# Mamba-2 block and feed-forward on one core: decay mask on GpSimd, differences for four heads at once, scores copied by ScalarE, and a new order on all engines

## The chip, the cores and the metric

The kernel runs on one core of a Trainium2 chip. The metric is the device time of one execution in microseconds (us), given as the median of the runs. The core has five engines that take their instructions in order from queues of their own and wait for each other by semaphores: TensorE (PE, with its weight loads PEld), VectorE (DVE), ScalarE (ACT), GpSimd (POOL) and SyncE (SP), which here only issues DMA transfers.

## The reference, cut to what matters

Input u is 4 x 1024 x 256, float32. Two layers, each with a residual:

```python
x = x + layernorm(mamba2(layernorm(x)))      # 8 heads of 64, state 128, conv of 4 taps
x = x + layernorm(ffn(layernorm(x)))         # width 2048, 4-bit weights, gelu(gate) * up, then down
# inside mamba2, for each chunk:
seg  = cs[..., :, None] - cs[..., None, :]   # cs: running sum of dt * A
Lmat = exp(where(tril, seg, -inf))           # decay matrix of each head
Y_diag = einsum(C, B, Lmat, x * dt)
states = einsum(B, exp(cs_last - cs), x * dt)
Y_off  = einsum(C, previous states, exp(cs))
y = (Y_diag + Y_off + x * D) * silu(z);  y = y * rsqrt(mean(y * y) + eps) * norm_weight
```

The kernel takes chunks of 128 time steps. For a chunk it needs, for every head, the matrix exp(cs[l] - cs[s]) for s <= l and zero elsewhere, multiplied by the scores B[s].C[l].

## The kernel before

**Tiling.** The 4096 time steps are treated in blocks of 512, shifted by half a block, so that there are 9 blocks (`NBLK`), the first and the last of them half. A block has two halves (j = 0, 1) of 256 steps, a half two tiles (q = 0 to 3 in the block) of 128. Iteration i runs the Mamba part of block i and the feed-forward part of block i - 1 interleaved.

**Order.** Every engine has its own written list of steps: `FIRST` for the start (blocks 0 and 1 and the half of block 2), `ORDER` for the iterations 2 to 8, `LAST` for the last feed-forward. A step is `name:k`; a trailing `<` means that it belongs to the block before (all feed-forward steps in `ORDER`), `>` to the next. `drive` walks the lists. No engine can leave its order, so a step that waits holds up everything written behind it on that engine.

**Feed-forward steps** (16 of each, n = 0 to 15): `gu:n` on TensorE makes the gate and the up product of 128 hidden columns (six matmuls of 512 columns each), `gelu:n` on ScalarE (L710) reads the gate bank, `inter:n` on VectorE (L999) multiplies it with the up bank, `split:n` on ScalarE (L717) and on GpSimd (L588) makes the high and low parts, `dn:n` on TensorE adds the down product (12 matmuls). Gate and up banks turn in a ring of three: gate n takes the bank that `inter:n-2` has read, up n the bank that `gelu:n-1` has read.

**Mamba steps of a half**, as far as the change touches them:
- `ip` projections and `taps` (ScalarE, L660 and L663), `conv` (VectorE, L881 to L901: a copy of the history, six multiply-adds at L890, a copy back), `silu` (ScalarE, L670). conv:1 with silu:1 gives x, conv:2 with silu:2 gives B and C of the first half, 4 and 5 those of the second.
- `softplus` gives dt * A; `cs` (TensorE, L1123) sums it along time; `decays` (VectorE, L843) copies the result to `csr`; SyncE stores that as rows in memory (L485) and spreads them over all partitions into `lmat`, one transfer of 512 KB for each tile (L493); `ct` (TensorE, L1127) transposes it; `sums` (VectorE, L850 to L855) collects `ct_`.
- `decay_sums:k` (four heads each) subtracts cs[s] in place in `lmat` and takes the minimum with 0 (VectorE, L864; for three of the four halves in `FIRST` on ScalarE, L643: 12 of 64 groups). `decay_matrix:k` (ScalarE, L652) takes the exponential. `exps` (L634) takes that of `ct_`.
- `gb` (TensorE, L1152) makes the scores and transposes B. `gb_copy` on VectorE (L873) copies the scores, multiplied by the 0/1 triangle `upto`; `gb_copy` on ScalarE (L685) copies the transposed B. `decayed_products:q` (VectorE, L909) multiplies `lmat` by the scores of the tile; this also zeroes what lies above the diagonal.
- `xtr`, `xdt` (x * dt), `yo` (TensorE, L1172: from the state), `yd:q` (TensorE, L1182: the diagonal part; waits for `decayed_products:q` and `xdt:q`), `st` (L1191), `ydiag`, `yt`, `out`, `stats2`, `ln2`, `x1n`.

ScalarE loads a table when it changes between gelu, silu and exponential (ACT_TABLE_LOAD).

Of the kernel before, what the change touches and what calls it, by code (L numbers as in the profile page):

```python
# [47 lines left out]
TINY = 1e-30  # L48

# [1233 lines left out]
```

## Time and profile before

| | us |
|---|---|
| median of 3 runs | 967.86 (967.83 to 968.83) |
| the profiled execution, its own time | 965.19 |
| its span, first to last instruction | 963.1 |
| TensorE busy (weight loads) | 880.5 (767.2) |
| VectorE busy | 751.7 |
| ScalarE busy | 614.1 |
| GpSimd busy | 355.0 |
| mean granted TensorE clock | 0.972 of full speed |

All times of single instructions come from the one profiled execution. An iteration of `ORDER` shows as a period of 109.4 us: its first gate product starts at 179.2, 288.3, 397.9 us and so on. In a timeline row the first number is the start, the second the time from the first instruction's start to the last one's end, `x6` the number of instructions merged; the brackets give the idle time in front and who ended it.

### The profile page before, as it was taken

To read this page: it belongs to the slowest core of one execution; us is meant where nothing else is said; L and a number is where in the kernel's file an instruction comes from. 1 tells how busy PE (TensorE), PEld (TensorE's weight loads), DVE (VectorE), ACT (ScalarE), POOL (GpSimd) and SP (SyncE) were. 2 spreads that over 40 slices of the span, in tenths; PEclk is the share of its full clock that TensorE was granted. 3 is DMA by queue.
4 is the path that set the end of the run, shared out by engine and by line. 5 is a ranking of instruction groups with operands and counts; after the bars stand their busy time and mean duration, and the time that the engine had idled before them with its cause. 6 is when DMAs were issued, how large, how long until landed. Compare 5 with 4: busy or idle time off the path is not lost.

```text
span 963.1 us, 17495 instructions
## 1 busy us (share of the span) xinstructions
PE 880.5 (91%) x6304; PEld 767.2 (80%) x6304; DVE 751.7 (78%) x2031; ACT 614.1 (64%) x1031; POOL 355.0 (37%) x342
## 2 busy tenths in 40 slices
PE   3256979999999999999999999999999999999987
PEld 3136878978897887988898897888888898888886
DVE  5989889877888697887978788787978878786232
ACT  5767777866749394765858385774858485673222
POOL 2030515253342516243442515243442525344323
PEclk9579999999999999999999999999999999999999
DMA  7502010200101010100102010110102010010000
GB/s 228 178 1 56 1 56 2 67 1 21 37 13 66 1 56 2 57 21 13 45 12 67 1 56 1 36 43 13 45 13 67 1 56 1 23 45 1 1 23 11
DMA packets 19205, 34.57 MB, mean 36 GB/s; under 512 B 2480, under 2 KB 11440, under 8 KB 19120
## 3 DMA queue, kind: packets, MB, share of 16 engines
q1 hardware_dynamic: 18256, 33.44, 10.8%
q8 instruction: 50, 0.82, 0.3%
q14 instruction: 35, 0.29, 0.1%
q10 hardware_dynamic: 864, 0.03, 0.1%
HBM read 29.14 MB, written 4.33 MB: 35 GB/s over the span
## 4 chain that ended last, share of the span: by engine, by line
PE 63%; DVE 15%; ACT 13%; issue 5%; POOL 3%; DMA 1%; SPq 0%; POOLq 0%; ACTq 0%; DVEq 0%
PE fb L1082 28%; PE db L1082 14%; PE mb L1082 10%; DVE xc L890 3%; PE mb L1191 3%; ACT L710 3%; PE mb L1182 2%; POOL hl L588 2%; ACT hid L710 2%; PE mb L1172 2%; ACT xc L670 2%; PE mb L1197 1%; ACT xc L663 1%; DVE st L1007 1%; ACT lmat L652 1%
## 5 line engine op out<-in xcount | busy, mean ns | idle before, releaser
L588 POOL TENSOR_TENSOR hl<-hid,hl 128x512 fp32r<-128x512 f32 (+1 forms) x144 | 182.7, 1273 | 336.1 <-ACT hl L717 336.1
L1082 PE MATMUL fb<-x1t,wg 128*128 128x512 f32 (+1 forms) x864 | 215.9, 386 | 3.2 <-DVE x1t L993 2.7
L1082 PE MATMUL fb<-x1t,wu 128*128 128x512 f32 (+1 forms) x864 | 203.2, 371 | 16.3 <-ACT hid L710 16.3
L1082 PE MATMUL db<-wd,hl 128*128 128x256 f32 x1536 | 217.5, 291 | 0.7 <-POOL hl L588 0.7
L1082 PEld LDWEIGHTS db<-wd,hl 128*128 128x128 f32 x1536 | 196.2, 191 | 14.7 <-issue 9.8
L1082 PEld LDWEIGHTS fb<-x1t,wu 128*128 128x128 f32 x864 | 150.6, 190 | 51.5 <-ACT hid L710 25.4
L1082 PEld LDWEIGHTS fb<-x1t,wg 128*128 128x128 f32 x864 | 147.6, 191 | 36.4 <-issue 11.6
L710 ACT ACTIVATE hid<-fb 128x512 f32<-128x512 f32 (+1 forms) x144 | 78.5, 550 | 135.1 <-PE fb L1082 119.5
L890 DVE SCALAR_TENSOR_TENSOR xc<-raw,cw,xc 128x256 f32<-128x256 f32 x288 | 135.7, 539 | 6.8 <-ACT xc L663 4.8
L999 DVE TENSOR_TENSOR hid<-fb,hid 128x512 f32<-128x512 f32 (+1 forms) x144 | 90.1, 626 | 60.7 <-PE fb L1082 34.4
L558 POOL TENSOR_TENSOR rs<-ve,neg_half 128x1 f32<-128x1 f32 (+2 forms) x89 | 61.9, 696 | 175.6 <-DVE ve L792 68.5
L717 ACT ACTIVATE hl<-hid 128x512 fp32r<-128x512 f32 (+1 forms) x144 | 82.1, 580 | 56.9 <-DVE hid L999 40.1
L710 ACT ACT_TABLE_LOAD x65 | 83.4, 1283 | 25.3 <-POOL hl L588 24.5
L1082 PE MATMUL mb<-xnt,wi 128*128 128x256 f32 x576 | 79.5, 289 | 13.8 <-ACT sz L678 9.0
L1082 PEld LDWEIGHTS mb<-xnt,wi 128*128 128x128 f32 x576 | 74.3, 195 | 15.3 <-issue 14.7
L567 POOL TENSOR_TENSOR xdd<-xdt,ex 128x512 f32<-128x512 f32 x32 | 34.4, 1076 | 82.4 <-ACT ex L634 64.9
L1082 PE MATMUL mb<-wi,xnt 128*128 128x264 f32 (+1 forms) x384 | 52.3, 285 | 0.2 <-ACT xc L663 0.2
L1082 PE MATMUL mb<-wo,yt 128*128 128x256 f32 x384 | 51.6, 283 | 0.0
L864 DVE TENSOR_SCALAR lmat<-lmat,ct_ 128x128 f32<-128x128 f32 x208 | 51.6, 316 | 0.0
L1082 PEld LDWEIGHTS mb<-wo,yt 128*128 128x128 f32 x384 | 47.9, 189 | 1.8 <-issue 1.0
L663 ACT ACTIVATE xc<-mb,cb,cw 128x256 f32<-128x256 f32 x96 | 49.2, 573 | 0.0
L1082 PEld LDWEIGHTS mb<-wi,xnt 128*128 128x128 f32 x384 | 48.3, 189 | 0.4 <-issue 0.4
(141 smaller groups left out, 1294.1 us busy)
## 6 DMA issues: line engine op xcount, KB each, us to landing
lmat<-rows SPq DMA_DIRECT2D x32, 512.0 KB, 4.5
xin<-in_u SPq DMA_DIRECT2D x16, 256.0 KB, 2.7
out<-xb SPq DMA_DIRECT2D x16, 256.0 KB, 2.3
wg_raw<-in_packed SPq DMA_DIRECT2D x4, 256.0 KB, 12.4
wg_raw<-in_scales SPq DMA_DIRECT2D x4, 256.0 KB
...
```

What stands on the lines that cost most here:

```text
L558: pool.tensor_tensor(dst, src, neg_half[:, 0:src.shape[1]], ALU.pow).then_inc(s["rstd" + name], 1)
L567: pool.tensor_tensor(per_head(xdd[:]), per_head(xdt[:]), spread_heads(ex[:, q // 2, 1, q % 2, :]), ALU.mult).then_inc(s["xdd"], 1)
L588: pool.tensor_tensor(hl[:, hs, n % 2, 1, :], hid[:, hs, n % 2, :], hl[:, hs, n % 2, 0, :].bitcast(F32), ALU.subtract).then_inc(s["lo"], 1)
L663: last = act.activation(xc[:, ct, :], ps[:, e, :], ACT.Identity, bias=cb[:, ct:ct + 1], scale=cw[:, ct, TAPS - 1:TAPS])
L670: act.activation(xc[:, 2 * pr:2 * pr + 2, :], xc[:, 2 * pr:2 * pr + 2, :], ACT.Silu).then_inc(s["xc"], 1)
L710: act.activation(hid[:, halves(f), n % 2, :], by_half(f_bank["gate", n], f), ACT.Gelu_apprx_tanh).then_inc(s["gelu"], 1)
L717: act.activation(hl[:, halves(f), n % 2, 0, :], hid[:, halves(f), n % 2, :], ACT.Copy).then_inc(s["hi"], 1)
L864: last = dve.tensor_scalar(lmat[:, c, h0 + h, :], lmat[:, c, h0 + h, :], ct_[:, 0, r:r + 1], 0.0, ALU.subtract, ALU.min)
L890: ins = dve.scalar_tensor_tensor(out=xc[:, ct, :], in0=raw[:, slot, e, tap:tap + SUB], scalar=cw[:, ct, tap:tap + 1], in1=xc[:, ct, :], op ...
L999: dve.tensor_tensor(hid[:, halves(f), n % 2, :], by_half(f_bank["up", n], f), hid[:, halves(f), n % 2, :], ALU.mult).then_inc(s["inter"], 1)
L1082: last = pe.matmul(ps, lhs(a, k), rhs(b, k), start=start and n == 0, stop=stop and n == len(todo) - 1, skip_group_check=check)
L1191: pe.matmul(m_bank["st", q][:], gb[:, 2 + c, :], xdd[:], start=True, stop=True).then_inc(s["st"], 1)
```

## The change

- `mask:q`, new on GpSimd, for each tile: waits for the tile's spread rows and writes -1e30 into `lmat` where s > l (columns 0 to 126 of all 8 heads, in place, affine_select).
- `decay_sums` on VectorE: one tensor_tensor for four heads in place of four tensor_scalar; no minimum any more. It and the ScalarE form wait for the mask.
- VectorE's `gb_copy` is gone: ScalarE copies the scores unmasked together with the transposed B, 512 columns. `decayed_products` waits for that copy.
- The lists of all engines in `ORDER` and `FIRST` are new, and TensorE's and ScalarE's in `LAST`.

```diff
+FAR = -1e30
...
 ORDER = {
     "pe": """
-        gu:0< gu:1< cs:0 gu:2< ct:0 dn:0< gu:3< xtr:0 gu:4< dn:1< gb:0 dn:2< gu:5< yo:0 yd:0 dn:3< st:0 gu:6<
-        yt:0 xtr:1 dn:4< out:0 yo:1 dn:5< yd:1 st:1 gu:7< xt:1 yt:1 gu:8< ip:3 out:1 z:3 z:4 dn:6< gu:9< dn:7<
-        ip:4 cs:1 ip:5 gu:10< ct:1 z:5 gu:11< gu:12< dn:8< gb:1 yo:2 dn:9< xtr:2 xt:0> gu:13< dn:10< yd:2 dn:11<
-        st:2 yt:2 xtr:3 gu:14< out:2 yo:3 dn:12< yd:3 st:3 gu:15< yt:3 dn:13< x1t:0 out:3 z:0> z:1> dn:14<
+        gu:0< cs:0 gu:1< gu:2< dn:0< ct:0 gu:3< xtr:0 gb:0 yo:0 dn:1< yd:0 dn:2< gu:4< st:0 yt:0 xtr:1 gu:5<
+        out:0 dn:3< yo:1 gu:6< yd:1 gu:7< st:1 xt:1 dn:4< yt:1 ip:3 gu:8< out:1 z:3 z:4 dn:5< ip:4 gu:9< cs:1
+        ip:5 dn:6< ct:1 dn:7< gu:10< z:5 gu:11< gb:1 yo:2 xtr:2 dn:8< dn:9< gu:12< xt:0> yd:2 st:2 dn:10< gu:13<
+        yt:2 xtr:3 gu:14< dn:11< out:2 yo:3 dn:12< yd:3 gu:15< st:3 yt:3 dn:13< x1t:0 out:3 z:0> z:1> dn:14<
         dn:15< ip:0> x1t:1 ip:1> z:2> ip:2>""",
     "act": """
-        gelu:0< gelu:1< split:0< silu:0 gelu:2< silu:1 gate:2 split:1< split:2< gelu:3< silu:2 gelu:4< exps:0
-        decay_matrix:0 decay_matrix:1 decay_matrix:2 split:3< split:4< gb_copy:0 decay_matrix:3 gelu:5< split:5<
-        yt_split:0 square:0 gelu:6< gelu:7< yt_split:1 split:6< xn_split:1 split:7< taps:3 square:1 gelu:8<
-        gate:3 gate:4 dt_bias:1 gelu:9< split:8< taps:4 taps:5 gelu:10< split:9< gate:5 gelu:11< silu:3 silu:4
-        silu:5 decay_matrix:4 decay_matrix:5 split:10< gb_copy:1 exps:1 decay_matrix:6 gelu:12< split:11<
-        xn_split:0> decay_matrix:7 square:2 gelu:13< yt_split:2 split:12< gelu:14< split:13< gelu:15< split:14<
-        square:3 yt_split:3 split:15< dt_bias:0> gate:0> x1_split:0 gate:1> x1_split:1 taps:0> taps:1> taps:2>""",
+        gelu:0< gelu:1< split:0< gelu:2< silu:0 silu:1 split:1< gate:2 silu:2 decay_matrix:0 decay_matrix:1
+        gb_copy:0 split:2< exps:0 gelu:3< square:0 gelu:4< yt_split:0 split:3< decay_matrix:2 decay_matrix:3
+        split:4< gelu:5< gelu:6< split:5< xn_split:1 gelu:7< yt_split:1 split:6< square:1 taps:3 gelu:8<
+        dt_bias:1 split:7< gate:3 gate:4 taps:4 gelu:9< taps:5 split:8< split:9< gelu:10< silu:3 silu:4 silu:5
+        gate:5 gelu:11< exps:1 gb_copy:1 split:10< decay_matrix:4 decay_matrix:5 split:11< gelu:12< xn_split:0>
+        decay_matrix:6 gelu:13< yt_split:2 square:2 decay_matrix:7 split:12< split:13< gelu:14< gelu:15<
+        split:14< yt_split:3 split:15< square:3 dt_bias:0> x1_split:0 gate:0> taps:0> x1_split:1 gate:1> taps:1>
+        taps:2>""",
     "dve": """
-        inter:0< decays:0 inter:1< conv:1 inter:2< conv:2 sums:0 xdt:0 decay_sums:0 inter:3< decay_sums:1
-        inter:4< gb_copy:0 decay_sums:2 decay_sums:3 decayed_products:0 stats1:1 yoff:0 ydiag:0 inter:5<
-        decayed_products:1 state:0 yt_split:0 xdt:1 stats2:0 xn:1 yoff:1 ln2:0 ydiag:1 inter:6< inter:7< state:1
-        yt_split:1 xn_split:1 stats2:1 dt_bias:1 ln2:1 conv:3 softplus:1 inter:8< stats1:0> decays:1 inter:9<
-        conv:4 inter:10< xn:0> conv:5 sums:1 inter:11< decay_sums:4 decay_sums:5 decay_sums:6 gb_copy:1
-        decayed_products:2 xdt:2 yoff:2 inter:12< x1n:0 xn_split:0> decay_sums:7 ydiag:2 decayed_products:3
-        x1n:1 state:2 yt_split:2 xdt:3 inter:13< stats2:2 yoff:3 inter:14< ln2:2 ydiag:3 state:3 yt_split:3
-        inter:15< stats2:3 x1n:2 dt_bias:0> ln2:3 softplus:0> x1n:3 fin:0< x1_split:0 x1_split:1 conv:0> ln4:0<""",
+        decays:0 inter:0< conv:1 inter:1< conv:2 sums:0 decay_sums:0 decay_sums:1 inter:2< xdt:0
+        decayed_products:0 stats1:1 yoff:0 ydiag:0 inter:3< decay_sums:2 state:0 yt_split:0 xdt:1 inter:4< xn:1
+        decay_sums:3 stats2:0 decayed_products:1 yoff:1 ln2:0 inter:5< ydiag:1 state:1 inter:6< xn_split:1
+        yt_split:1 inter:7< conv:3 stats2:1 dt_bias:1 ln2:1 softplus:1 conv:4 decays:1 inter:8< inter:9<
+        stats1:0> conv:5 sums:1 inter:10< decay_sums:4 decay_sums:5 inter:11< x1n:0 xdt:2 decay_sums:6 xn:0>
+        decayed_products:2 yoff:2 xn_split:0> ydiag:2 decay_sums:7 inter:12< state:2 yt_split:2 xdt:3 inter:13<
+        decayed_products:3 stats2:2 inter:14< yoff:3 ln2:2 ydiag:3 inter:15< x1n:1 yt_split:3 x1n:2 state:3
+        stats2:3 dt_bias:0> ln2:3 softplus:0> x1n:3 fin:0< x1_split:0 x1_split:1 conv:0> ln4:0<""",
     "pool": """
-        split:0< split:1< split:2< xdt:0 split:3< yoff:0 split:4< stats1:1 split:5< stats2:0 xdt:1 yoff:1
-        split:6< split:7< ln2:0 stats2:1 stats1:0> split:8< split:9< split:10< xdt:2 yoff:2 split:11< ln2:1
-        split:12< xdt:3 stats2:2 yoff:3 split:13< ln2:2 split:14< split:15< stats2:3 ln2:3 fin:0<""",
+        split:0< mask:0 mask:1 split:1< split:2< xdt:0 yoff:0 split:3< stats1:1 stats2:0 split:4< xdt:1 yoff:1
+        ln2:0 split:5< split:6< stats2:1 split:7< split:8< split:9< stats1:0> mask:2 mask:3 ln2:1 split:10<
+        split:11< xdt:2 yoff:2 split:12< xdt:3 stats2:2 split:13< yoff:3 split:14< ln2:2 split:15< stats2:3
+        ln2:3 fin:0<""",
...
+            def mask(i, par, q):
+
+                c = q % 2
+                pool.wait_ge(rows_spread[c], 16 * halves_before(i, q // 2) + 16)
+                pool.affine_select(out=lmat[:, c, :, 0:CH - 1], in_=lmat[:, c, :, 0:CH - 1], compare_op=ALU.is_ge,
+                                   fill=FAR, base=0, pattern=[[0, HEADS], [1, CH - 1]],
+                                   channel_multiplier=-1).then_inc(s["masked"], 1)
+
...
                 c, h0 = k // 2 % 2, 4 * (k % 2)
                 act.wait_ge(s["sums"], count("sums", i, k // 4))
+                act.wait_ge(s["masked"], count("masked", i, k // 2))
                 for h in range(4):
                     r = HEADS * c + h0 + h
                     last = act.activation(lmat[:, c, h0 + h, :], lmat[:, c, h0 + h, :], ACT.Relu,
...
             def gb_copy(i, par, j):
-                act.wait_ge(s["gm"], count("gm", i, j))
-                act.activation(gb[:, 2:4, :].rearrange("p a l -> p (a l)"), m_bank["gb", j][:, SUB:],
-                               ACT.Copy).then_inc(s["gbs"], 1)
+                act.wait_ge(s["gb"], count("gb", i, j))
+                if isinstance(i, int) and i == 0:
+                    act.wait_ge(wi_z_ready, 1)
+                wait_before(act, "m", i, 2 * j - 1)
+                act.activation(gb[:].rearrange("p a l -> p (a l)"), m_bank["gb", j][:], ACT.Copy).then_inc(s["gbs"], 1)
 
...
                 c, h0 = k // 2 % 2, 4 * (k % 2)
                 dve.wait_ge(s["sums"], count("sums", i, k // 4))
-                for h in range(4):
-                    r = HEADS * c + h0 + h
-                    last = dve.tensor_scalar(lmat[:, c, h0 + h, :], lmat[:, c, h0 + h, :],
-                                             ct_[:, 0, r:r + 1], 0.0, ALU.subtract, ALU.min)
-                last.then_inc(s["upto_s"], 1)
-
-            def gb_copy(i, par, j):
-
-                dve.wait_ge(s["gb"], count("gb", i, j))
-                if isinstance(i, int) and i == 0:
-                    dve.wait_ge(wi_z_ready, 1)
-                dve.tensor_tensor(gb[:, 0:2, :], m_bank["gb", j][:, 0:SUB].rearrange("p (c l) -> p c l", c=2),
-                                  upto[:].unsqueeze(1).broadcast_to([P, 2, CH]), ALU.mult).then_inc(s["gm"], 1)
+                r = HEADS * c + h0
+                dve.wait_ge(s["masked"], count("masked", i, k // 2))
+                dve.tensor_tensor(lmat[:, c, h0:h0 + 4, :], lmat[:, c, h0:h0 + 4, :],
+                                  ct_[:, 0, r:r + 4].unsqueeze(2).broadcast_to([P, 4, CH]),
+                                  ALU.subtract).then_inc(s["upto_s"], 1)
...
                 c = q % 2
                 dve.wait_ge(s["lmat"], count("lmat", i, 2 * q + 1))
-                dve.wait_ge(s["gm"], count("gm", i, q // 2))
+                dve.wait_ge(s["gbs"], count("gbs", i, q // 2))
                 dve.tensor_tensor(lmat[:, c, :, :], lmat[:, c, :, :],
                                   gb[:, c, :].unsqueeze(1).broadcast_to([P, HEADS, CH]), ALU.mult).then_inc(s["m"], 1)
```

In `FIRST` (its diff is left out) GpSimd's new list begins `stats1:1 wi_split:0 stats1:0> mask:2 xdt:2 yoff:2 mask:3 xdt:3 stats2:2 yoff:3 ln2:2 stats2:3 ln2:3 stats1:1> mask:0> mask:1> split:0 xdt:0> yoff:0> split:1`; the others move conv, dequantization and copies of the weights against the Mamba steps. In `LAST` single down products and splits move by one place.

## Rows read from the trace of the kernel before

**Rows 1.** The page, chain that ended last, shares of the span by engine.
```profile
PE 63%; DVE 15%; ACT 13%; issue 5%; POOL 3%; DMA 1%; SPq 0%; POOLq 0%; ACTq 0%; DVEq 0%
```

**Rows 2.** Windows (length; PE, PEld, DVE, ACT, POOL busy; clock; DMA): start-up, steady iteration, short one.
```profile
0.00:179.20 179.20, 119.99 (x922) 104.53 (x923) 152.57 (x385) 128.23 (x250) 51.06 (x63) 0.87 0.23 72
288.60:398.00 109.40, 107.11 (x765) 92.84 (x764) 89.86 (x250) 72.57 (x115) 43.20 (x39) 1.00 0.09 30
835.50:919.70 84.20, 80.18 (x512) 68.12 (x510) 48.23 (x118) 39.27 (x61) 31.00 (x27) 1.00 0.06 20
```

**Rows 3.** Waits from 288.7 to 398.1: us in total, times, longest.
```profile
PEld fb L1082 <- ACT hid L710: 3.4, 3, 1.5
...
PE fb L1082 <- ACT hid L710: 2.1, 3, 1.1
```

**Rows 4.** Timeline of TensorE in the iteration from 288.3.
```profile
288.28 1.55 PE L1082 MATMUL fb<-x1t,wg 128*128 128x512 f32 x6
...
291.04 1.52 PE L1082 MATMUL fb<-x1t,wg 128*128 128x512 f32 x6
292.97 1.65 PE L1082 MATMUL fb<-x1t,wu 128*128 128x512 f32 x6 [0.41 <-ACT hid L710]
...
313.22 1.15 PE L1182 MATMUL mb<-xdt,lmat 128*64 128x64 f32 x32
...
367.84 1.15 PE L1182 MATMUL mb<-xdt,lmat 128*64 128x64 f32 x32
```

**Rows 5.** Groups of instructions by line and shape: busy us, mean ns, idle before.
```profile
L710 ACT ACT_TABLE_LOAD x65 | 83.4, 1283 | 25.3 <-POOL hl L588 24.5
...
L864 DVE TENSOR_SCALAR lmat<-lmat,ct_ 128x128 f32<-128x128 f32 x208 | 51.6, 316 | 0.0
...
L873 DVE TENSOR_TENSOR gb<-mb,upto 128x256 f32<-128x256 f32 x16 | 6.6, 414 | 0.5 <-PE mb L1155 0.5
...
L685 ACT ACTIVATE gb<-mb 128x256 f32<-128x256 f32 x16 | 5.9, 369 | 0.0
...
L541 POOL MEMSET state<- 128x512 f32 x1 | 0.5, 524 | 0.0
...
L538 POOL TENSOR_SCALAR_AFFINE_SELECT ident<-ident 128x128 f32<-128x128 f32 x1 | 0.3, 292 | 0.2 <-POOL ident L537 0.2
```

**Rows 6.** Timeline of VectorE in the same iteration.
```profile
292.95 0.69 DVE L999 TENSOR_TENSOR hid<-fb,hid 128x512 f32<-128x512 f32 x1 [0.61 <-ACT hid L710]
294.88 0.29 DVE L843 COPY csr<-mb 128x128 f32<-128x128 f32 x1 [1.24 <-PE mb L1123]
...
295.88 2.46 DVE L890 SCALAR_TENSOR_TENSOR xc<-raw,cw,xc 128x256 f32<-128x256 f32 x6
298.38 0.17 DVE L901 COPY hist<-raw 128x6 f32<-128x6 f32 x1
...
299.26 3.50 DVE L890 SCALAR_TENSOR_TENSOR xc<-raw,cw,xc 128x256 f32<-128x256 f32 x6
302.80 1.15 DVE L901 COPY hist<-raw 128x6 f32<-128x6 f32 x1
...
308.33 0.69 DVE L999 TENSOR_TENSOR hid<-fb,hid 128x512 f32<-128x512 f32 x1 [0.74 <-ACT hid L710]
...
311.63 1.21 DVE L909 TENSOR_TENSOR lmat<-lmat,gb 128x1024 f32<-128x1024 f32 x1
...
360.17 1.23 DVE L909 TENSOR_TENSOR lmat<-lmat,gb 128x1024 f32<-128x1024 f32 x1
```

**Rows 7.** Timeline of GpSimd in the same iteration.
```profile
301.19 2.72 POOL L588 TENSOR_TENSOR hl<-hid,hl 128x512 fp32r<-128x512 f32 x2 [5.51 <-ACT hl L717]
...
360.26 2.27 POOL L588 TENSOR_TENSOR hl<-hid,hl 128x512 fp32r<-128x512 f32 x1 [8.71 <-ACT hl L717]
```

**Rows 8.** SyncE's issue of the spread rows, and landing times of lmat's transfers.
```profile
296.58 0.82 SPq L493 DMA_DIRECT2D lmat<-rows  x2
...
DMA to landing us min/median/max: 3.8/4.2/4.7
```

More of the change, by code:

```diff
@@ L137 @@
[L137 to L145 removed]
+        stats1:1 xn:1 wi_split:0 xn_split:1 rates:0 conv:3 dq:0 dt_bias:1 dq:1 conv:4 stats1:0> conv:5 scale:0
@@ new lines @@
+        wo_split:0 xn:0> scale:1 dq:2 dq:3 wo_lo:0 softplus:1 dq:4 scale:2 decays:1 scale:3 xdt:2 dl:0 dq:5 dq:6
+        scale:4 dl:1 dl:2 scale:5 sums:1 scale:6 yoff:2 decayed_products:2 state:2 dq:7 xn_split:0> ydiag:2 dq:8
+        yt_split:2 scale:7 xdt:3 stats2:2 decayed_products:3 yoff:3 ln2:2 ydiag:3 state:3 dq:9 x1n:2 yt_split:3
+        dl:4 dq:10 stats2:3 dt_bias:0> ln2:3 softplus:0> x1n:3 conv:0> decays:0> x1_split:1 conv:1> stats1:1>
+        dl:5 inter:0 sums:0> conv:2> scale:8 dl:6 xdt:0> inter:1 yoff:0> decayed_products:0> state:0> dl:3
@@ new lines @@
+        ydiag:0> scale:9 inter:2 yt_split:0> xn:1> inter:3 xdt:1> stats2:0> decayed_products:1> yoff:1> ln2:0>
+        inter:4 ydiag:1> xn_split:1> state:1> scale:10 yt_split:1> dl:7 inter:5 dq:11 stats2:1> dl:9 dt_bias:1>
+        ln2:1> x1n:0> softplus:1> inter:6 conv:3> decays:1> inter:7 conv:4> conv:5> sums:1> inter:8 dl:10
+        stats1:0>> dl:8 inter:9 xn:0>> xdt:2> yoff:2> decayed_products:2> ydiag:2> inter:10 decayed_products:3>
+        xn_split:0>> scale:11 inter:11 yt_split:2> inter:12 state:2> xdt:3> inter:13 yoff:3> stats2:2> ydiag:3>
@@ new lines @@
+        ln2:2> yt_split:3> dl:11 state:3> x1n:1> inter:14 stats2:3> inter:15 dt_bias:0>> ln2:3> softplus:0>>
+        x1n:2> x1n:3> conv:0>> x1_split:0> x1_split:1> fin:0 ln4:0""",
+    "pool": """
+        stats1:1 wi_split:0 stats1:0> mask:2 xdt:2 yoff:2 mask:3 xdt:3 stats2:2 yoff:3 ln2:2 stats2:3 ln2:3
+        stats1:1> mask:0> mask:1> split:0 xdt:0> yoff:0> split:1 xdt:1> stats2:0> split:2 yoff:1> split:3 ln2:0>
+        split:4 split:5 stats2:1> split:6 split:7 mask:2> ln2:1> split:8 stats1:0>> mask:3> xdt:2> split:9
+        yoff:2> split:10 split:11 split:12 xdt:3> yoff:3> stats2:2> split:13 ln2:2> stats2:3> split:14 split:15
+        ln2:3> fin:0""",
@@ L187 @@
                 decay_sums=4, decay_matrix=4, ip=3, taps=3, conv=3, silu=3, z=3, gate=3, gb=1, gb_copy=1,
-                decayed_products=2, xtr=2, xdt=2, yo=2, yoff=2, yd=2, st=2, state=2, ydiag=2, square=2, yt=2,
+                decayed_products=2, mask=2, xtr=2, xdt=2, yo=2, yoff=2, yd=2, st=2, state=2, ydiag=2, square=2, yt=2,
                 yt_split=2, out=2, stats2=2, ln2=2, x1n=2, x1t=1, x1_split=1)
@@ L593, in fin @@
                 rstd("4", rs4[:, at], ve4[:, at], f, 0)
-            drive(pool, "pool", dict(wi_split=wi_split, stats1=stats1, stats2=stats2, xdt=xdt_, yoff=yoff, ln2=ln2, split=split, fin=fin), consts)
+            drive(pool, "pool", dict(wi_split=wi_split, stats1=stats1, stats2=stats2, mask=mask, xdt=xdt_, yoff=yoff, ln2=ln2, split=split, fin=fin), consts)
         @block.scalar
```

74 lines of the change are left out of this document (28 added, 46 removed).

## The prediction, made before the changed kernel was run

> **What bounds the kernel now.** I read the page's chain first [rows 1], then the busy time by stage [rows 2], then one steady iteration in order of time on each engine [rows 4 to 8]. The reader is to see that TensorE is the bound, but not all through. In the steady iteration it is busy 107.1 of 109.4 us at full clock, and six such iterations and a shorter one (84.2 us) fill 740 us of the span. Ahead of them lies a start-up of 179.2 us, in which TensorE works 120 us and VectorE 152.6: it is bound by VectorE and by chains. The chain that ended last runs 63% over TensorE and 28% over VectorE and ScalarE: TensorE takes its steps in a written order, so whoever delivers late makes it wait, and that time is lost, since its queue has nothing to spare.
>
> What TensorE loses in a steady iteration: three waits, all of an "up" product for ScalarE's gelu of the step before, whose bank it takes. They are 2.1 us by the matmul row and 3.4 by the weight-load row [rows 3]; I take 2.7, the mean. The first of them stays in any order that begins alike: gate 1 starts at 291.04 and up 1 at 292.97 where 1.4 would do, because gelu 0 ends late [rows 4]. It is 0.5 us. So removing all that can be removed would give 2.2 us an iteration, some 15 us over seven. That is the ceiling of the gain in the steady part, whatever VectorE saves.
>
> **The change, part by part.**
> *Differences.* Four tensor_scalar of 128x128 become one tensor_tensor of 128x512, 52 times (the other 12 groups are on ScalarE and stay). The four took 51.6 / 208 x 4 = 1.0 us of busy time [rows 5]; the one is between half of the 1.21 us of the 128x1024 product with two inputs in SBUF and the 0.69 us of a 128x512 product fed from PSUM [rows 6]: I take 0.65. Saved: 0.35 each, 2.8 us an iteration, on VectorE.
> *Scores.* VectorE's masked copy goes, 0.41 us twice an iteration; ScalarE's copy grows from 256 to 512 columns, at most by another 0.37 us [rows 5]. So VectorE works 89.9 - 3.6 = 86 of 109 us. This is beside TensorE's work and worth nothing in itself; only an earlier result on which TensorE waits counts.
> *Table loads.* Counting the changes between gelu, silu and exponential in ScalarE's written order, I find 21 in an iteration before and 19 after; at 1.28 us a load [rows 5] that is 2.6 us less on an engine that is busy 72.6 of 109.4 [rows 2]. Again worth only what a late gelu costs.
> The Trainium skill, ScalarE: Activation LUTs, What ACT_TABLE_LOAD costs, puts a switch at about 2.66 us in all, a drain included; by that ScalarE would gain 5.3 us. In the trace a gelu starts right behind the 1.28 us, and no term below uses it.
> *Masks.* GpSimd gets 32 affine_selects over 8 x 127 elements. Its only like is 0.29 us for 128 elements [rows 5]. By proportion 1016 elements cost 2.3 us, the upper bound; the lower is that of a memset, which only writes, 0.52 us for 512, so 1.0. Part of the 0.29 must be fixed, so I take the middle, 1.6 us: 6.6 us an iteration on an engine with 43.2 busy. GpSimd's own load is no limit. What is queued behind the masks is: split 1 (then down product 1 on TensorE), and VectorE's differences, which now wait for rows, then mask.
>
> *New waits.* VectorE's differences wait for a mask, and behind them stand inter:2, xdt:0 and the decayed product, for which yd:0 waits. The decayed product now waits for ScalarE's copy of gb:0, and ScalarE's own queue behind that copy (split 2, exps, gelu 3) waits for gb:0 too; so a late gb:0 holds up the next bank read and down product 2. The copy's wait for the half before is long over.
>
> *Where this falls.* The new order moves the first half's scan forward. Before, its diagonal product (yd:0) starts at 313.22, 24.9 us after the iteration's first gate at 288.28 [rows 4]. In the new list it stands behind four gate/up pairs of 2.76 us (two starts apart, 288.28 to 291.04), two down products of 1.4, and cs, ct, xtr, gb, yo, together 2.1: 11.0 + 2.9 + 2.1 + the 0.5 wait = 16.5 us. TensorE asks for it 8 us sooner. Can VectorE deliver? From gelu 0's multiplication at 292.95 to the end of the decayed product at 312.84 it needed 19.9 us [rows 6]. Off that come its waits for others (1.24 and 0.74), two multiplications that now stand later (1.2), the masked copy (0.35), the second tile's eight differences (2.0), the saving on the first tile's two groups (0.7), csr (0.2), and the 2.0 us by which conv and history copy were stretched (below): 11.5 us. 292.95 + 11.5 - 288.28 = 16.2 us. So the new order fits to some tenths, provided that nothing is stretched.
>
> *The stretch.* A conv chain of six takes 2.46 us alone, but 3.50 when GpSimd's splits begin in it at 301.19, and the small history copy behind it 1.15 instead of 0.17 [rows 6, 7]. GpSimd suffers too (a split of 1.36, half of that pair, took 2.27 at 360.26). So each GpSimd instruction that begins within VectorE's SBUF work costs VectorE about 1.0 of its 1.36 us. In the new order, after csr (VectorE is free at 292.34, where its idle time of 0.61 before 292.95 begins, and cs:0 is done before), the rows land as late after csr as before: 294.88 to 296.58 plus 4.2 [rows 6, 8], 5.9 us, thus at 298.3 to 298.7. Conv 1 runs from 293.6 and meets split 0 (294.4): +1.0. Conv 2 then runs from 298 to 301, exactly where both masks come: 1.6 us each, by the same proportion +1.2 each, rising to 1.5 as they come back to back behind one another. Silu 2 waits for conv 2, gb:0 for silu 2 (1.2 us of room), yd:0 for all. Sum: 1.0 + 1.5 + 1.5 = 4.0 us late at yd:0; with split 1 behind the masks hitting too, 5.0; with nothing colliding, 0; with 2.3 us masks 5.5 to 6.5. I take 4.0.
> The Trainium skill, SBUF (State Buffer), Who interferes with whom, has the shared port pair held for the whole instruction, and counts an operation with two SBUF inputs as a contender. By it each mask costs its full 1.6 and each split 1.36: 5.9 us with split 1, an iteration 1.9 us worse than my 4.0 and a time of some 998. The 3.50 and 1.15 rows agree with its kind, with 1.0 measured for its 1.36.
>
> *The rest of the iteration.* In the second half there is room: before, decayed product 2 ended at 361.4, 6.4 us ahead of yd:2 at 367.84 [rows 4, 6]. Counted from cs:1, the new list asks for yd:2 2.6 us sooner (two down products stand ahead of it where a gate/up pair, a down product and a gelu wait of 1.3 stood: 2.9 against 5.5), and xdt:2 (1.3) is now done first: 2.5 us stay, so masks 2 and 3, some 2.5 us of stretch together, cost little. The two other gelu waits lose table loads ahead of them. I leave 0.5 us for what contention does in all of this. The tail of all four lists is nearly unchanged. So an iteration loses 0.5 + 4.0 + 0.5 = 5.0 where it lost 2.7: +2.3, over seven iterations (the short one has the same front) +16.
>
> *Start-up.* Three copies leave VectorE (-1.2 us), six masks come (6 x 1.6, on a GpSimd that is busy 51 of 179 us [rows 2]), all differences there stay on ScalarE. If every mask hit VectorE at 1.2, +7.2 - 1.2 = +6; if they fall into waits, -1. The order of dequantization is also new: within +-4. I take +1. The closing feed-forward is TensorE steps back to back: 0.
>
> Sum: +17. The profiled execution took 965.2 (span 963.1), so 982; the median of the runs stands 2.7 higher, at 967.9, so 985.
>
> **Rivals.**
> 1. *The collisions miss or are absorbed: faster.* If rows land when VectorE is in PSUM-fed work, or GpSimd takes turns without holding it, yd:0 is on time and the gelu waits are gone: -2.2 an iteration, -15, and -1 at the start: 952; half of that 960. For it: the count above closes to 0.1 us, and VectorE has 3.6 us less to do. Against: rows 6 and 7, and conv 2 stands where the rows land. It decides below 2.2 us of lateness at yd:0. Chance 0.30.
> 2. *It cancels.* Lateness of 2 to 2.5 us takes the place of the removed waits: 966 to 970. Chance 0.10.
> 3. *Masks at the upper bound.* 2.3 us each: split 1 ends some 1.4 later, down product 1 waits too, 6 us late at yd:0, +4.3 x 7 = 30, and start-up +5: 1003. Chance 0.08.
> 4. *The forecast*, 975 to 997: 0.52.
>
> **How the numbers follow.** 0.2%, 1.9 us, is what a measurement here can tell from no change. Faster is rival 1, 0.30; same rival 2, 0.10; slower forecast and rival 3, 0.60. The range leaves out the better part of rival 1 (below 954, some 0.12) and rival 3: 954 to 998. The likeliest case's own range is 975 to 997.
>
> **What would show it.** In the profile after: masks of about 1.6 us; conv chains of over 4 us under the first two masks, where one takes 2.46 alone; TensorE waiting before gb:0 (for silu) and yd:0 (for the decayed product), together some 4 us, each iteration; a steady iteration of 111.7 us instead of 109.4; two table loads fewer in it; VectorE busy less in differences but not in all. The prediction is wrong if the iteration is under 109.4, if conv keeps its 2.46 us beside the masks, or if TensorE's wait moves to a gelu or a split that I took as covered.

## The result, and the profile after

The changed kernel took 991.83 us (985.68 to 994.21), the kernel before beside it 967.85: a ratio of 1.0245, 95% interval 1.0210 to 1.0281. It is slower, as forecast, and 6.8 us above the predicted 985. The profiled executions differ by 24.9 us in span (988.0 against 963.1), and the accounts below are of these. One execution of e7 below had a granted clock of 0.65 throughout and took 1273 us; it is left out of that run's time.

The page of the kernel after: busy shares, and the chain that ended last by engine (before: [rows 1]).
```profile
PE 888.4 (90%) x6304; PEld 774.6 (78%) x6304; DVE 774.6 (78%) x1859; ACT 603.5 (61%) x1016; POOL 405.5 (41%) x374
...
PE 51%; DVE 31%; issue 7%; ACT 6%; DMA 1%; POOL 1%; DVEq 0%; SPq 0%; POOLq 0%; ACTq 0%
```
TensorE's share of the chain fell from 63% to 51%, VectorE's rose from 15% to 31%: more of the time that ended last was spent waiting for VectorE. Windows after, in the columns and for the stages of [rows 2]:
```profile
0.00:185.60 185.60, 125.03 (x922) 107.44 (x923) 157.14 (x382) 129.94 (x251) 60.95 (x69) 0.85 0.22 69
297.60:409.90 112.30, 107.21 (x764) 93.18 (x763) 93.39 (x224) 71.00 (x113) 49.36 (x43) 1.00 0.09 29
858.70:942.80 84.10, 79.94 (x512) 68.54 (x510) 46.50 (x98) 36.07 (x58) 33.43 (x28) 1.00 0.06 20
```
In the iteration TensorE does the same 107.2 us of work, but in 112.3 us; VectorE, which was to get 3.6 us lighter, is busy 93.4 where it was 89.9. By the first gate product of each iteration the 24.9 us fall so: the start-up ends at 185.63 in place of 179.23 (+6.4); the six iterations to the last one's start take 673.1 in place of 656.1 (+17.0, or 112.2 each for 109.35); the rest takes 129.3 in place of 127.75 (+1.5).

Groups after: the masks, and the conv chains (before: 135.7 us, mean 539).
```profile
L577 POOL TENSOR_SCALAR_AFFINE_SELECT lmat<-lmat 128x1016 f32<-128x1016 f32 x32 | 39.1, 1230 | 47.4 <-DMA lmat<-rows 46.5
L896 DVE SCALAR_TENSOR_TENSOR xc<-raw,cw,xc 128x256 f32<-128x256 f32 x288 | 156.3, 610 | 13.8 <-ACT xc L675 12.7
```
The conv chains alone gained 20.6 us of busy time, with not one instruction more. One place shows it. Timeline of VectorE and then of GpSimd, in the iteration that starts at 297.58:
```profile
302.22 3.50 DVE L896 SCALAR_TENSOR_TENSOR xc<-raw,cw,xc 128x256 f32<-128x256 f32 x6
...
306.64 5.17 DVE L896 SCALAR_TENSOR_TENSOR xc<-raw,cw,xc 128x256 f32<-128x256 f32 x6
...
312.38 1.29 DVE L878 TENSOR_TENSOR lmat<-lmat,ct_ 128x512 f32<-128x512 f32 x2
...
315.53 1.23 DVE L915 TENSOR_TENSOR lmat<-lmat,gb 128x1024 f32<-128x1024 f32 x1
```
```profile
303.36 1.29 POOL L599 TENSOR_TENSOR hl<-hid,hl 128x512 fp32r<-128x512 f32 x1 [8.37 <-ACT hl L731]
307.27 2.45 POOL L577 TENSOR_SCALAR_AFFINE_SELECT lmat<-lmat 128x1016 f32<-128x1016 f32 x2 [2.62 <-DMA lmat<-rows]
309.70 1.44 POOL L599 TENSOR_TENSOR hl<-hid,hl 128x512 fp32r<-128x512 f32 x1
```
Conv 1 meets split 0 and takes 3.50 us, conv 2 meets both masks and split 1 and takes 5.17, where such a chain alone takes 2.46 [rows 6]. What TensorE then waits for, in its own timeline of the same iteration (all its waits on another engine):
```profile
312.53 0.71 PE L1158 MATMUL mb<-xc 128*128 128x128 f32 x4 [1.44 <-ACT xc L682]
...
316.86 1.15 PE L1188 MATMUL mb<-xdt,lmat 128*64 128x64 f32 x32 [1.11 <-DVE lmat L915]
...
334.89 1.65 PE L1088 MATMUL fb<-x1t,wg 128*128 128x512 f32 x6 [0.47 <-DVE hid L1005]
...
375.24 1.15 PE L1188 MATMUL mb<-xdt,lmat 128*64 128x64 f32 x32 [1.51 <-DVE t L932]
...
407.26 1.67 PE L1088 MATMUL mb<-wi,xnt 128*128 128x256 f32 x12 [0.57 <-ACT sz L690]
```
These are gb:0 (for silu 2, behind conv 2), yd:0, a gate product, yd:2 (for yoff:2 on VectorE, which stands right behind the decayed product) and z: 5.1 us, where before there were 2.1 us of gelu waits [rows 3]. The last two iterations (cs:0 at 747.62 and 861.44) differ: the masks begin later in conv 2, which takes 4.16 and 3.31 us, so gb:0 waits 0.44 us and then not at all; but the masks also end later, and yd:0 waits 1.86 and 2.44.

### The profile page after: what moved, and what is told of

Its sections match the earlier page's. It is cut to its first block, busy times and chain, and to the rows that moved or that the text cites. A ratio compares the mean times of both kernels' runs of the same rounds, so it can differ in the third digit from the quotient of the medians.

```text
span 988.0 us, 17451 instructions
## 1 busy us (share of the span) xinstructions
PE 888.4 (90%) x6304; PEld 774.6 (78%) x6304; DVE 774.6 (78%) x1859; ACT 603.5 (61%) x1016; POOL 405.5 (41%) x374
## 4 chain that ended last, share of the span: by engine, by line
PE 51%; DVE 31%; issue 7%; ACT 6%; DMA 1%; POOL 1%; DVEq 0%; SPq 0%; POOLq 0%; ACTq 0%
PE fb L1088 21%; DVE xc L896 12%; PE db L1088 12%; PE mb L1088 10%; PE mb L1197 3%; PE mb L1188 2%; DVE lmat L915 2%; DVE hid L1005 2%; ACT L724 1%; PE mb L1178 1%; ACT xc L675 1%; PE mb L1203 1%; DVE st L1013 1%; DVE xdt L924 1%; DVE mr L974 1%
## 5 line engine op out<-in xcount | busy, mean ns | idle before, releaser
L599 POOL TENSOR_TENSOR hl<-hid,hl 128x512 fp32r<-128x512 f32 (+1 forms) x144 | 187.5, 1303 | 361.7 <-ACT hl L731 360.6
L1088 PE MATMUL fb<-x1t,wg 128*128 128x512 f32 (+1 forms) x864 | 210.4, 379 | 7.7 <-DVE x1t L999 4.2
L1088 PEld LDWEIGHTS db<-wd,hl 128*128 128x128 f32 x1536 | 196.1, 192 | 17.1 <-issue 11.8
L896 DVE SCALAR_TENSOR_TENSOR xc<-raw,cw,xc 128x256 f32<-128x256 f32 x288 | 156.3, 610 | 13.8 <-ACT xc L675 12.7
L561 POOL TENSOR_TENSOR rs<-ve,neg_half 128x1 f32<-128x1 f32 (+2 forms) x89 | 68.4, 768 | 143.5 <-DVE ve L968 69.1
L1088 PE MATMUL mb<-wi,xnt 128*128 128x264 f32 (+1 forms) x384 | 55.4, 294 | 4.1 <-ACT sz L690 3.1
L577 POOL TENSOR_SCALAR_AFFINE_SELECT lmat<-lmat 128x1016 f32<-128x1016 f32 x32 | 39.1, 1230 | 47.4 <-DMA lmat<-rows 46.5
L1188 PEld LDWEIGHTS mb<-xdt,lmat 128*64 128x64 f32 x1024 | 33.8, 141 | 28.9 <-issue 27.8
L1088 PEld LDWEIGHTS mb<-wi,xnt 128*128 128x128 f32 x384 | 50.9, 196 | 6.9 <-issue 6.0
L1188 PE MATMUL mb<-xdt,lmat 128*64 128x64 f32 x1024 | 37.9, 228 | 18.9 <-DVE lmat L915 10.4
L947 DVE TENSOR_TENSOR yg<-mb,yg 128x512 f32<-128x512 f32 x32 | 22.1, 692 | 41.4 <-POOL yg L587 41.1
```

The costliest lines, as they stand in the source:

```text
L561: pool.tensor_tensor(dst, src, neg_half[:, 0:src.shape[1]], ALU.pow).then_inc(s["rstd" + name], 1)
L577: pool.affine_select(out=lmat[:, c, :, 0:CH - 1], in_=lmat[:, c, :, 0:CH - 1], compare_op=ALU.is_ge, fill=FAR, base=0, pattern=[[0, HEADS] ...
L599: pool.tensor_tensor(hl[:, hs, n % 2, 1, :], hid[:, hs, n % 2, :], hl[:, hs, n % 2, 0, :].bitcast(F32), ALU.subtract).then_inc(s["lo"], 1)
L896: ins = dve.scalar_tensor_tensor(out=xc[:, ct, :], in0=raw[:, slot, e, tap:tap + SUB], scalar=cw[:, ct, tap:tap + 1], in1=xc[:, ct, :], op ...
L947: dve.tensor_tensor(yg[:], m_bank["yd", q][:], yg[:], ALU.add).then_inc(s["ydiag"], 1)
L1088: last = pe.matmul(ps, lhs(a, k), rhs(b, k), start=start and n == 0, stop=stop and n == len(todo) - 1, skip_group_check=check)
```

## The experiments

Each time stands beside runs of the kernel before on the same chip (966.8 to 967.6 us). "Iteration" is the mean distance from one cs:0 to that of the next iteration, "start" the time of the first 512-column gate product, both from the profiled execution.

**e1: without the masks.** `mask` is taken out of GpSimd's lists, and the waits for it.
```
-                                  ALU.subtract).then_inc(s["upto_s"], 1)
+                                  ALU.min).then_inc(s["upto_s"], 1)
```


> The changed kernel with its order kept and GpSimd's 32 masks left out (nothing above the diagonal is suppressed); the difference of four heads takes the minimum of its two inputs instead of subtracting, with the same operands and shape, so that the exponentials stay finite. Theory A (masks stretch VectorE's conv 2, and that makes TensorE late): conv 2 goes from 5.2 us to 2.5 to 3.6, TensorE's waits before gb:0 (1.4) and yd:0 (1.1) go, an iteration falls from 112.2 to about 109.5, the time to 968 to 976. Rival B (the new order asks too early whatever the masks do): the two waits stay over 2 us together and the time is 985 or more.


968.83 us, ratio 1.0019 (1.0003 to 1.0036); iteration 109.2, start 182.7. The masks make the whole iteration's loss, 3.0 us. Timeline of VectorE and of TensorE in e1, in the iteration that starts at 291.42 (conv 2, gb:0 and yd:0):
```profile
300.51 3.50 DVE L895 SCALAR_TENSOR_TENSOR xc<-raw,cw,xc 128x256 f32<-128x256 f32 x6
```
```profile
304.75 0.69 PE L1157 MATMUL mb<-xc 128*128 128x128 f32 x4
...
309.06 1.15 PE L1187 MATMUL mb<-xdt,lmat 128*64 128x64 f32 x32 [1.11 <-DVE lmat L914]
```
Conv 2 still meets split 1. The wait at gb:0 (1.44) is gone, and so is the one at yd:2 (1.51): together these are the 3.0 us. But yd:0 waits the same 1.11 us as with the masks, where Theory A had this wait go too, and the gate and z wait 0.46 and 0.59. So 2.2 us of waits belong to the new order itself, as many as the 2.1 of gelu that it removed: with all that it saves VectorE it stands only where the old kernel stood.

**e2: the mask as an instruction that only writes.**
```
-                pool.affine_select(out=lmat[:, c, :, 0:CH - 1], in_=lmat[:, c, :, 0:CH - 1], ...
+                pool.memset(lmat[:, c, :, 0:CH - 1], FAR).then_inc(s["masked"], 1)
```


> The changed kernel with each mask as a memset of the same 8 x 127 columns: GpSimd writes lmat but reads nothing (the decay matrix becomes zero in these columns). Theory A1 (VectorE and GpSimd collide only where GpSimd reads SBUF): conv 2 is stretched by split 0 or 1 alone, to at most 3.6 us, and the time is that of the kernel without masks, 968 to 977. Theory A2 (any GpSimd instruction on lmat stretches VectorE by its length, here about 0.95 us each): conv 2 takes about 4.6 us and the time is 984 to 990. Rival B: no change from 992.


972.67 us, ratio 1.0078 (1.0048 to 1.0109); iteration 109.2, start 186.2. The memset takes 0.95 us at the mask's place and over the same columns. Timeline of VectorE, then of GpSimd, in e2:
```profile
304.29 2.46 DVE L894 SCALAR_TENSOR_TENSOR xc<-raw,cw,xc 128x256 f32<-128x256 f32 x6
```
```profile
304.89 0.95 POOL L577 MEMSET lmat<- 128x1016 f32 x1 [2.59 <-DMA lmat<-rows]
306.12 0.95 POOL L577 MEMSET lmat<- 128x1016 f32 x1 [0.28 <-DMA lmat<-rows]
```
Conv 2, from 304.29 to 306.75, lies over the first and two thirds of the second and keeps its 2.46 us. So neither the wait nor GpSimd's time costs the iteration anything: what costs is the instruction that reads SBUF beside VectorE. The memset is also another and a shorter instruction (0.95 us for 1.23); that it is the reading rests on the splits as well, which read and stretch a conv too [rows 6, 7]. Most of the 3.8 us by which e2 is slower than e1 lies in the start-up (186.2 against 182.7).

**e3: the mask twice**, one behind the other, the first with a semaphore of its own.


> The changed kernel with every mask done twice, one behind the other. Theory A: conv 2 meets another 2.4 us of GpSimd's work, so that yd:0 comes some 2 us later still and an iteration takes 114 to 115.5; with the start-up the time is 1008 to 1020. Rival B: GpSimd has time for it, so the time stays below 1000.


1028.29 us, ratio 1.0633 (1.0604 to 1.0663); iteration 116.6. The second mask costs 4.4 us an iteration where the first cost 3.0, and the time is above what both theories allowed. In its trace the granted clock falls to 0.5 seven times between the cs:0 at 196.4 and the one at 896.0, in the changed kernel once; e4 shows what such a fall costs. By e4's 2.7 us each (an estimate) the six more make 2.7 of the 4.4 us.

**e4: the new order with the old operations.** The lists of the changed kernel without masks, in the kernel before; VectorE's gb_copy:0 stands behind inter:2, gb_copy:1 behind inter:11.


> The new order on all engines with the kernel before's operations: no masks, four tensor_scalar with a minimum for each difference, VectorE's masked score copy back in its list (ahead of the decayed products). Theory A after the first runs (the order alone wins nothing, and only GpSimd's reading masks lose): an iteration of 109.5 to 111, with TensorE's wait before yd:0 0.5 to 1 us longer than the 1.1 of the kernel without masks because VectorE's front has some 0.7 us more to do; time 970 to 980. Rival E (the new order is the gain and the operations eat it): below 962.


991.81 us, ratio 1.0257 (1.0241 to 1.0272): expected 970 to 980. Its iterations are not alike: 116.7, 113.7, 110.9, 113.5, 113.6, 110.9 us. Timeline of TensorE in e4, in the second of them, and windows of 2 us there (TensorE's granted clock is the third figure from the end):
```profile
315.96 1.97 PE L1187 MATMUL mb<-xdt,lmat 128*64 128x64 f32 x32 [2.67 <-DVE lmat L914]
317.86 2.93 PE L1087 MATMUL db<-wd,hl 128*128 128x256 f32 x12
```
```profile
312.00:314.00 2.00, 1.29 (x11) 1.08 (x10) 2.00 (x5) 1.93 (x5) 0.48 (x1) 1.00 0.00 0
314.00:316.00 2.00, 0.04 (x2) 0.07 (x3) 2.00 (x2) 1.47 (x2) 2.00 (x2) 0.87 0.00 0
316.00:318.00 2.00, 2.00 (x33) 1.88 (x33) 1.92 (x7) 0.00 (x0) 1.76 (x2) 0.50 0.04 8
318.00:320.00 2.00, 2.00 (x10) 2.00 (x11) 0.61 (x2) 0.00 (x0) 1.28 (x1) 0.50 0.00 0
320.00:322.00 2.00, 2.00 (x8) 1.71 (x8) 1.97 (x5) 0.72 (x2) 0.00 (x0) 0.50 0.00 0
```
TensorE waits 2.67 us for the decayed product, which took 2.24 us because it began 0.1 us behind split 2. The granted clock drops to 0.50, the 1.2 GHz level, and stays there for over 6 us: yd:0 takes 1.97 us where it takes 1.15 [rows 4], a down product 2.93 where it takes 1.70. What such a drop costs is seen in two other iterations of e4, whose yd:0 waits just as long:
```profile
429.63 1.15 PE L1187 MATMUL mb<-xdt,lmat 128*64 128x64 f32 x32 [2.68 <-DVE lmat L914]
...
540.54 1.83 PE L1187 MATMUL mb<-xdt,lmat 128*64 128x64 f32 x32 [2.68 <-DVE lmat L914]
```
Behind the first the clock stays full, and its iteration takes 110.9 us; behind the second it falls, and that one takes 113.5. The iteration of 116.7 us has two drops, the other one of 110.9 none. So a drop costs some 2.7 us on top of the wait, and the wait's length alone doesn't decide on it. Without the drops the order costs +1.5 us an iteration with these operations, with them +3.8.

**e5: the old order with the new operations.** ORDER, FIRST and LAST of before, no gb_copy on VectorE; masks 0 and 1 behind split 2, masks 2 and 3 behind stats1:0 of the next pass.


> The kernel before's order on all engines with all of the new operations: masks 0 and 1 stand behind split 2, masks 2 and 3 behind stats1 of the next block; VectorE's score copy is gone. Theory A: masks 0 and 1 run beside VectorE's PSUM-fed multiplications, the front loses nothing, and VectorE has 3.6 us less to do: TensorE's waits stay at 2 to 3 us an iteration (109 to 109.5) and the time is 962 to 970. Rival C (the operations are bad in any order: masks on GpSimd late for the differences and in splits' way): 975 or more.


1023.06 us, ratio 1.0593 (1.0570 to 1.0615); iteration 117.6. This I placed badly: masks 2 and 3 stand ahead of split 8 and wait 5.1 us for their rows, so ScalarE's gelu is late and an up product waits 4.02 us at 376.17; the clock falls there too, once in every iteration, and its six matmuls take 2.93 us. That is far outside Theory A; e7 moves these two masks behind split 9.


> The kernel before's order on all engines with the new operations, as in the run before, but masks 2 and 3 behind split 9, and not ahead of split 8, which they held up until the rows had landed. Theory A: the 4.0 us wait of up 13 for gelu goes, an iteration falls from 117.6 to 109.5 to 113 and the time from 1023 to 972 to 993. Rival C (the operations cost as much in any place): an iteration of 116 or more.


988.50 us, ratio 1.0218 (1.0199 to 1.0237), inside Theory A's range. Its trace can't be used, so e11 is the same kernel once more.


> The kernel of e7 once more, for its trace alone: the old order with the new operations, masks 0 and 1 behind split 2 and masks 2 and 3 behind split 9. Theory A: the iteration is 110.5 to 112.5 us, the convs beside the masks are stretched to 3.3 us or more, up:1 no longer waits, and the start-up ends 5 us or more late. Rival K (the clock alone makes it slower, by waits of 2.5 us or more that let it fall): the iterations without such a wait are 109.5 us, and those with one 2.5 to 6 us longer.


986.17 us, iteration 111.6, start 185.8. Rival K falls: between 160 us and the closing part at 940 no window lies below full clock. Theory A is half right. Conv 2 takes 3.49 us, but for a split, as before; the masks fall on a small copy behind it (1.06 us for 0.16). The up products still wait, 1.8 us. And yd:0 waits 1.18 us, with this ahead of it on VectorE:
```profile
321.73 1.33 DVE L919 TENSOR_TENSOR lmat<-lmat,gb 128x1024 f32<-128x1024 f32 x1 [2.82 <-ACT gb L704]
```

**e6: the old start with the new order.** FIRST of the kernel before, with the masks put in.


> The changed kernel with FIRST from the kernel before, its three pairs of masks put ahead of the scan step that needs them; ORDER and LAST as changed. Theory A: iterations as in the changed kernel, about 112.2; the start-up, 7 us longer in the changed kernel (first gate product of the second stage at 185.6 against 178.6), comes back by 3 to 6 us, so 984 to 989. Rival F (the masks and not the start's new order lengthen the start-up): the start-up stays at 184 or more and the time at 990 or more.


992.11 us, ratio 1.0271 (1.0244 to 1.0299), start 185.7: Rival F. With the masks in it the old start is no shorter than the new one (185.6). As its steps are those of before in the same order, the two can be laid side by side. Timeline of VectorE in e6, and of GpSimd:
```profile
47.84 2.12 DVE L797 TENSOR_TENSOR wo<-wo_raw,wo 128x1024 fp32r<-128x1024 f32 x1
49.88 2.11 DVE L1061 TENSOR_TENSOR wg<-wg_raw,wg 128x1024 fp32r<-128x1024 f32 x1
...
104.73 1.23 DVE L918 TENSOR_TENSOR lmat<-lmat,gb 128x1024 f32<-128x1024 f32 x1 [2.08 <-ACT gb L703]
...
143.39 4.15 DVE L899 SCALAR_TENSOR_TENSOR xc<-raw,cw,xc 128x256 f32<-128x256 f32 x6 [1.53 <-ACT xc L678]
```
```profile
47.15 3.78 POOL L580 TENSOR_SCALAR_AFFINE_SELECT lmat<-lmat 128x1016 f32<-128x1016 f32 x2 [17.39 <-DMA lmat<-rows]
...
99.46 2.16 POOL L580 TENSOR_SCALAR_AFFINE_SELECT lmat<-lmat 128x1016 f32<-128x1016 f32 x2
...
144.00 1.24 POOL L580 TENSOR_SCALAR_AFFINE_SELECT lmat<-lmat 128x1016 f32<-128x1016 f32 x1 [0.64 <-DMA lmat<-rows]
```
The first pair meets two products of weights that take 1.22 us each before: +1.8. In the second pair the first mask ends 2 us after ScalarE was ready for its differences, and the scores' copy waits behind them: TensorE's yd:0 is 3.7 us late by then. The third meets a conv: +1.7. Each pair of masks in the start-up found something on the chain. By 158 us the lag is 6.0 us.

**e8: masks 0 and 1 behind split 1** in the changed kernel's ORDER.


> The changed kernel with masks 0 and 1 behind split 1 in ORDER's GpSimd list and nothing else moved. Theory A: conv 2 meets split 1 and perhaps one mask and takes 3.5 to 4.7 instead of 5.2 us, TensorE's wait before gb:0 (1.4) falls below 0.5; the differences wait for the masks instead, so yd:0 gains 0.3 to 1 us in all; iteration 111.2 to 112, time 984 to 991. Rival G (the masks' lateness costs more than their collision): iteration over 112.6, time over 993.


997.63 us, ratio 1.0318 (1.0301 to 1.0336). Rival G. Conv 2 takes 3.51 us instead of 5.17, but the masks then fall on two small copies behind it (0.95 and 1.07 us for 0.17) and end 11.8 us after cs:0 instead of 9.4, and yd:0 waits 2.56 us at 323.57, with the clock at 0.50 behind it.

**e9: the old order, new operations, no masks** (e7 with e1's edit).


> The orders (FIRST, ORDER, LAST) of the kernel before, with the changed operations, but without GpSimd's masks; the four-head difference is a min instead of a subtract, so the decay above the diagonal isn't left out of the output. It completes the square: new order with the same operations took 968.8 us, the old order with its own operations 967.9. Theory A (in the new order the gain of the lighter VectorE operations was used up by asking for yd:0 earlier): in the old order yd:0 is asked for late, the wait ahead of up 1 goes when the masked copy of gb no longer stands on VectorE, and an iteration falls from 109.4 to 107 to 109; 950 to 966 us. Rival H (TensorE's waits of the old order don't hang on these operations: the waits of 2.7 us in an iteration that remained were on other things): 966 to 970 us. Rival O (the old order fits the new operations badly, ScalarE's wider copy and its place behind the fourth exponential): 975 us or more.


974.85 us, ratio 1.0085 (1.0068 to 1.0101); iteration 110.4, start 180.9. No theory had it: Rival O has the kind, not the size. yd:0 waits 1.19 us, and the decayed product 2.82 us for ScalarE's copy of gb:0, as in e11. In the old list of ScalarE that copy stands behind three exponentials and two splits; the old kernel could bear it, since VectorE copied its half itself.

**e10: yd:0 and yd:2 later on TensorE.**
```
-  gu:3< xtr:0 gb:0 yo:0 dn:1< yd:0 dn:2< gu:4< st:0 ...       xt:0> yd:2 st:2 dn:10< gu:13<
+  gu:3< xtr:0 dn:1< gb:0 yo:0 dn:2< gu:4< yd:0 st:0 ...       xt:0> dn:10< yd:2 st:2 gu:13<
```


> The changed kernel with another order on TensorE alone, in ORDER: dn:1 stands ahead of gb:0, yd:0 behind dn:2 and gu:4, and yd:2 and st:2 behind dn:10. Theory A (what the masks cost in an iteration is that gb:0, yd:0 and yd:2 are asked for 1.4, 1.1 and 1.5 us before they can be had): these waits go, an iteration falls from 112.2 to 108.5 to 110.5, and the whole to 965 to 982 us. Rival L (the work behind yd:0 needs its result as early: st:0, yt:0, out:0 and ydiag:0 then come 3 us late, and the waits only move there, or gu:4 is held by the gelu that stands behind the exponentials on ScalarE): 988 to 1000 us.


1012.01 us, ratio 1.0456 (1.0431 to 1.0482); iteration 114.2. In the iteration shown the waits at gb:0, yd:0 and yd:2 did go. But dn:2 needs split 2, which GpSimd ends 17.6 us after cs:0, here as in the changed kernel. There yd:0 and its wait stand ahead of dn:2 and fill the time; here TensorE asks for dn:2 at 14.1 us and waits:
```profile
319.86 2.93 PE L1088 MATMUL db<-wd,hl 128*128 128x256 f32 x12 [3.52 <-POOL hl L599]
```
The clock falls behind it. Rival L named the kind of thing, a wait that only moves, and the wrong step. One list moved alone turned three short waits into one long one.

**e12: the copy earlier in the old order.**
```
-        exps:0 decay_matrix:0 decay_matrix:1 decay_matrix:2 split:3< split:4< gb_copy:0 decay_matrix:3
+        gb_copy:0 exps:0 decay_matrix:0 decay_matrix:1 decay_matrix:2 split:3< split:4< decay_matrix:3
```


> The kernel of e11 (old order, new operations, masks behind splits 2 and 9) with one token moved in ScalarE's list of ORDER: gb_copy:0 stands ahead of exps:0 and no longer behind split 4. In e11 the first decayed product (321.73) waits 2.82 us for that copy, and yd:0 stands 1.18 us; in e9 it is 2.82 and 1.19. Theory C (that wait is all that the old order loses by the scores' copy on ScalarE): yd:0 no longer waits, an iteration falls from 111.6 to 110.2 to 110.8, and the whole from 986 to 988 to 975 to 982 us. Rival D (the copy then waits for gb:0 itself, or pushes the exponentials and the next gelu back by its 0.57 us, so that an up product waits instead): an iteration of 111.2 us or more, 984 us or more.


979.62 us, ratio 1.0135 (1.0116 to 1.0155); iteration 110.4, and yd:0 doesn't wait: Theory C. It is the fastest of the kernels with the masks, 12 us ahead of the changed one, and still 13 behind the kernel before. No version tried beats that one.

The square (us; iteration, start):

| | old order | new order |
|---|---|---|
| old operations | 967.9; 109.4, 179.2 | 991.8 (e4); 113.2, 180.1 |
| new, no masks | 974.9 (e9); 110.4, 180.9 | 968.8 (e1); 109.2, 182.7 |
| new, masks | 986.2 (e11); 111.6, 185.8 | 991.8; 112.2, 185.6 |
| new, masks, copy first | 979.6 (e12); 110.4, 187.7 | not tried |

## Why the prediction held, and where its terms were off

**The mechanism.** It was that masks read SBUF beside conv 2, that conv 2 delays gb:0 and yd:0, and that this outweighs the removed gelu waits. The trace, e1 and e2 show the stretch and the delay: no masks, no loss; a mask that doesn't read, no stretch and no loss in the iteration. The weighing was another one. Of the 5.1 us of waits the masks made 1.44 in the first half, where 3.0 were predicted, and 1.51 in the second, where nearly nothing was. The other 2.2 us stand in e1 too: with nothing colliding the change was to win 2.2 us an iteration, and without masks, with splits 0 and 1 still in the convs, it won 0.2. That the iteration came out near the forecast is in part luck.

**The masks' length.** 1.23 us each, for 1.6 taken (bounds 1.0 to 2.3). Conv 1 grew by 1.04 us as said. Conv 2 grew by 2.71, for the 4.0 of both masks (3.0) and split 1 (1.0); against e1's 3.50, which has the split alone, the two masks cost it 1.67. So this term was nearly twice too large. The chain lay beside 3.9 us of GpSimd's work, and VectorE lost 0.7 us for each us of it. The Trainium skill, SBUF (State Buffer), Who interferes with whom, calls the shared port pair an exclusive lock; by that, as an estimate, conv 2 would lose all 3.9. The trace and e2 agree with the page on who contends, and the trace not on the amount.

**yd:0.** It came 19.3 us after the iteration's first gate, for 16.5 + 4.0. The waits there are 1.44 + 1.11 = 2.55 us, for 4.0: this term was too large. TensorE's side was counted right: in e1 yd:0 starts at 17.6 us, 1.1 of them a wait, so TensorE asks for it at 16.5. On VectorE's side e1 has two stretches of 1.04 us, for splits 0 and 1, so without any it would have been ready at 15.6 us (an estimate), for 16.2.

**The second half** was wrong. "2.5 us stay, so masks 2 and 3 cost little", with 0.5 us left for contention: conv 5 took 5.26 us, and yd:2 waited 1.51. In the iterations from 525.6 and 636.7, where conv 5 took 4.42, yd:2 doesn't wait, and they are the ones of 111 us instead of 112.6; in e1 conv 5 takes 3.6 and yd:2 doesn't wait either. With z's 0.6 and a gate's 0.5, which e1 has too and the prediction hadn't, the sum came to 5.1 us of waits, where 5.0 were predicted, by errors that cancel. The gelu waits all went, also the one of 0.5 that was to stay.

**The iteration**: +2.8 us by six periods, for +2.3; +17.0 in all with the short one's extra 1.5, 18.5 for 16. Part of it is the clock, which no step had. Timeline of TensorE in the changed kernel's longest iteration (113.8 us), and windows there:
```profile
763.88 1.65 PE L1188 MATMUL mb<-xdt,lmat 128*64 128x64 f32 x32 [1.86 <-DVE lmat L915]
765.46 2.69 PE L1088 MATMUL db<-wd,hl 128*128 128x256 f32 x12
```
```profile
764.00:766.00 2.00, 2.00 (x34) 1.88 (x34) 1.46 (x7) 0.56 (x1) 2.00 (x3) 0.58 0.00 0
766.00:768.00 2.00, 2.00 (x13) 2.00 (x12) 0.00 (x0) 0.00 (x0) 2.00 (x2) 0.57 0.00 0
```
It fell once behind the start-up here, and never in the kernel before until its closing part.

**The start-up** is the largest error: +1 predicted, +6.4 measured. I took +1 between the bounds -1 and +6, and let the new order of dequantization carry the rest. The starts in the square divide it. Without masks the new operations start at 180.9 in the old order and 182.7 in the new, +1.7 and +3.5, where the copies taken off VectorE were to give back 1.2. The masks add 4.9 and 2.9. e6 shows how: all three pairs fell on the chain. Reading isn't all of it there, since a mask can also be what ScalarE waits for, and with e2's memsets the start is as late as with masks, 186.2. All this holds to some 2 us only: e6, e11 and e12 have the same start and operations, and start at 185.7, 185.8 and 187.7.

**What the order was for** follows from the square. As the lists stand, the new operations do better in the new order (e9 against e1: -6 us) and the old ones in the old (e4: +24). How much of the 6 us is one token can't be said: e12's move gave back 7 us in the old order with masks, and was not tried without them. Together, without masks, they come out within 0.2% of where they started: VectorE's savings, which I put at nothing in themselves, were in fact worth nothing there. The table loads fell from 21 to 19 an iteration, as counted, and the gelu waits went with them in the new order; which of the two did it, no run separates. The new waits of 2.2 us took their place.

**Open:** what the +3.5 us of e1's start consists of, and whether e2 really starts later than e1; one profile of each can't tell that from scatter. And when the clock falls: in the changed kernel it did after a wait of 1.86 us and not after one of 2.44 (yd:0 at 877.82, with the windows behind it at full clock), in e4 after one of 2.68 us and not after the other.
